# Output LayerNorm from the residual's accumulated sum and a squaring pass on ScalarE, biases by broadcast load, and another closing order

## What is computed

```
u     = h @ h.T / sqrt(384);  a = softmax(u);  delta = a * adj
attn  = delta / (sum(delta) + 1e-10)
ctx   = (attn * upper) @ (h @ Wl.T + bl) + diag(attn) * (h @ Ws.T + bs) + (attn * lower) @ (h @ Wr.T + br)
h     = relu(layernorm(ctx, eps=1e-12) * g + beta)
out   = layernorm(x + h_after_layer_2, eps=1e-5)       # no gain, no shift
```

## Time and profile before

| | |
|---|---|
| median of three runs | 1637.04 us (1635.62, 1637.04, 1637.73) |
| the profiled execution | 1637.5 us, span 1635.7 us |
| busy share PE, PEld, DVE, ACT, POOL | 98%, 98%, 91%, 58%, 73% |
| chain that ended last, by engine | PE 91%, DVE 2%, then DMA, POOL, SP's queue, ACT about 1% each |
| DMA | 178.61 MB, 43% of 16 engines |

### The profile page before, as it was taken

One profiled execution on the slowest core, in us unless ns is written; L12 is line 12 of the kernel. 1 busy time (PEld: TensorE's weight loads), 2 busy tenths in 40 slices (PEclk: granted clock), 3 DMA queues, 4 the chain that ended last, 5 costly groups with the idle time before them and its releaser, 6 DMA issues.

```text
span 1635.7 us, 35455 instructions
## 1 busy us (share of the span) xinstructions
PE 1609.5 (98%) x9505; PEld 1601.3 (98%) x9505; DVE 1491.4 (91%) x4628; ACT 951.4 (58%) x2451; POOL 1202.1 (73%) x1541
## 2 busy tenths in 40 slices
PE   8999999999999999999999999999999999999995
PEld 7999999999999999999999999999999999999995
DVE  7799999999999999999999999999999999999987
ACT  5565665556566556556656655665665556566553
POOL 5677777777777777777777777777777777777763
PEclk9999999999999999999999999999999999999998
DMA  4344444444444444444444444444444444444431
GB/s 158 94 116 107 111 111 112 106 113 114 107 114 109 111 107 113 114 107 114 110 110 107 112 115 107 114 111 110 108 111 115 107 114 111 110 109 110 114 83 44
DMA packets 463515, 178.61 MB, mean 109 GB/s; under 512 B 348545, under 2 KB 462593, under 8 KB 463490
## 3 DMA queue, kind: packets, MB, share of 16 engines
q1 hardware_dynamic: 463490, 178.32, 43.1%
HBM read 112.34 MB, written 65.86 MB: 109 GB/s over the span
## 4 chain that ended last, share of the span: by engine, by line
PE 91%; DVE 2%; DMA 1%; POOL 1%; SPq 1%; ACT 1%; issue 1%; DVEq 0%; POOLq 0%; ACTq 0%
PE p_proj L427 70%; PE p_gather L514 15%; PE p_score L421 5%; PE p_score L443 1%; DMA rows_mem<-rows_blocks 1%; DMA attnT_whole<-attn_mem 1%; SPq L366 1%; SPq L351 1%; POOL rstd L1164 0%; POOL proj_split L283 0%; POOL attnT L1154 0%; POOL attnT_split L1160 0%; DVE stats L626 0%; ACT normed L961 0%; DVE stats L672 0%
## 5 line engine op out<-in xcount | busy, mean ns | idle before, releaser
L427 PE MATMUL p_proj<-w,hT_layer 128*128 128x384 f32 x6912 | 1371.6, 339 | 0.2 <-DVE proj L697 0.2
L427 PEld LDWEIGHTS p_proj<-w,hT_layer 128*128 128x128 f32 x6912 | 1165.9, 189 | 0.5 <-DVE proj L697 0.5
L283 POOL TENSOR_TENSOR proj_split<-proj,proj_split 128x768 fp32r<-128x768 f32 x253 | 467.6, 1848 | 276.9 <-ACT proj_split L957 276.9
L957 ACT ACTIVATE proj_split<-proj 128x768 fp32r<-128x768 f32 x256 | 214.9, 839 | 394.9 <-DVE proj L697 393.8
L514 PE MATMUL p_gather<-proj_split,attnT_split 128*128 128x384 f32 x1536 | 309.2, 335 | 3.0 <-POOL attnT_split L1160 2.4
L514 PEld LDWEIGHTS p_gather<-proj_split,attnT_split 128*128 128x128 f32 x1536 | 270.0, 188 | 4.9 <-POOL attnT_split L1160 4.1
L1164 POOL TENSOR_TENSOR rstd<-veps,neg_half 128x1 f32<-128x1 f32 x384 | 211.2, 550 | 75.3 <-DVE veps L635 61.8
L697 DVE TENSOR_TENSOR proj<-p_proj,bias_all 128x768 f32<-128x768 f32 x256 | 245.1, 957 | 12.0 <-PE p_proj L427 4.4
L421 PE MATMUL p_score<-hT_layer 128*128 128x256 f32 x768 | 216.8, 283 | 2.0 <-DVE rows L729 2.0
L1154 POOL TENSOR_TENSOR attnT<-attnT_whole,sides 128x256 f32<-128x256 f32 x249 | 184.5, 741 | 41.0 <-DMA attnT_whole<-attn_mem 39.0
L1160 POOL TENSOR_TENSOR attnT_split<-attnT,attnT_split 128x256 fp32r<-128x256 f32 x256 | 190.3, 743 | 5.8 <-ACT attnT_split L948 5.8
(11 more groups left out here) (67 smaller groups left out, 1568.2 us busy)
## 6 DMA issues: line engine op xcount, KB each, us to landing
xt_raw<-xT SPq DMA_DIRECT2D x128, 192.0 KB, 2.5
xn<-x SPq DMA_DIRECT2D x128, 192.0 KB, 2.4
out<-o SPq DMA_DIRECT2D x128, 192.0 KB, 2.0
rows_mem<-rows_blocks SPq DMA_DIRECT2D x124, 192.0 KB, 1.9
rowsT<-rows_mem SPq DMA_DIRECT2D x496, 48.0 KB, 2.4
adj_layer<-adj SPq DMA_DIRECT2D x256, 64.0 KB, 1.9
attn_mem<-attn_blocks SPq DMA_DIRECT2D x124, 128.0 KB, 1.7
attnT_whole<-attn_mem SPq DMA_DIRECT2D x496, 32.0 KB, 2.2
```

What stands on the lines that cost most here:

```text
L283: op.tensor_tensor(proj_split[u][:, LO], proj[u][:, UP:LOW + 1, :], proj_split[u][:, HI].bitcast(F32), ALU.subtract).then_inc(s_proj_lo[k], 1)
L427: return nc.tensor.matmul(p_proj[:, which, 0:D], hT_of(k, b)[:, slot, st, c, :], w[:, k, which, mv, c, :], start=(n == 0), stop=(n == 8))
L957: nc.scalar.activation(proj_split[u][:, HI], proj[u][:, UP:LOW + 1, :], ACT.Copy).then_inc(s_proj_hi[k], 1)
```

## The change

The output statistics no longer come from bn_stats. The instruction that makes y also accumulates its sum per row; DVE scales that by -1/384 to the negated mean; ScalarE squares y + (-mean) with an accumulated sum and turns that into the variance plus epsilon. y gets two buffers, and `gathered` is no longer used for it. In the loop ScalarE runs the squaring where `finish` stood and `finish` after layer 2's cross scores; POOL's deviation for the output moves behind the one for layer 2. Both layers' biases are loaded with partition broadcasts, the sides' and the self bias apart, layer 1's behind its weights; the matmuls and copies that spread it go, and 9 warm matmuls run instead of 4. The closing steps have another order on DVE, ScalarE and POOL.

```diff
...
@@ -110,7 +108,11 @@
         normed = sb("normed", [P, D])
         stats6 = sb("stats6", [P, 3, 6])
         rows = [sb(f"rows{k}", [P, 4, COLS]) for k in (1, 2)]
-        y = sb("y", [P, D])
+        y = sb("y", [P, 2, D])
+        y_sum = sb("y_sum", [P, 1])
+        y_squares = sb("y_squares", [P, 1])
+        spread = sb("spread", [P, D])
+        out_eps = sb("out_eps", [P, 1])
 
 
 
...
@@ -317,12 +315,14 @@
         @block.sync
         def _(sp):
             sp.dma_start(xt_raw[:, 0], xT[0]).then_inc(s_xt[0], 16)
-            sp.dma_start(bias_row[:], bias[0:1]).then_inc(s_bias_row, 16)
             sp.dma_start(w_raw[:, 0, UP], WT[0, :, UP]).then_inc(s_w[0][UP], 16)
             sp.dma_start(adj_tile[0][:, 0], adj[0]).then_inc(s_adj[0][0], 16)
             sp.dma_start(w_raw[:, 0, LOW], WT[0, :, LOW]).then_inc(s_w[0][LOW], 16)
             sp.dma_start(xt_raw[:, 1], xT[1]).then_inc(s_xt[1], 16)
             sp.dma_start(w_raw[:, 0, SELF], WT[0, :, SELF]).then_inc(s_w[0][SELF], 16)
+            sp.dma_start(bias_all[:, 0, UP:LOW + 1],
+                         bias[0, UP:LOW + 1].partition_broadcast(P)).then_inc(s_bias_sides[0], 16)
+            sp.dma_start(bias_all[:, 0, SELF], bias[0, SELF].partition_broadcast(P)).then_inc(s_bias_self[0], 16)
             sp.dma_start(adj_tile[0][:, 1], adj[1]).then_inc(s_adj[0][1], 16)
             done(sp, s_lo[0], 0)
             sp.dma_start(xt_raw[:, 0], xT[2]).then_inc(s_xt[0], 16)
...
@@ -380,7 +380,10 @@
                         sp.dma_start(w_raw[:, 1, which], WT[1, :, which]).then_inc(s_w[1][which], 16)
                     sp.dma_start(gain1[:], gain_cols).then_inc(s_cols, 16)
                     sp.dma_start(shift1[:], shift_cols).then_inc(s_cols, 16)
-                    sp.dma_start(bias_all[:, 1], bias[1].partition_broadcast(P)).then_inc(s_bias2, 16)
+                    sp.dma_start(bias_all[:, 1, UP:LOW + 1],
+                                 bias[1, UP:LOW + 1].partition_broadcast(P)).then_inc(s_bias_sides[1], 16)
+                    sp.dma_start(bias_all[:, 1, SELF],
+                                 bias[1, SELF].partition_broadcast(P)).then_inc(s_bias_self[1], 16)
                     sp.dma_start(gain2[:], gain_row.partition_broadcast(P)).then_inc(s_const, 16)
                     sp.dma_start(shift2[:], shift_row.partition_broadcast(P)).then_inc(s_const, 16)
                 if live(i, i - 1):
...
@@ -518,13 +521,8 @@
 
 
             pe.wait_ge(s_warm, 1)
-            for n in range(4):
+            for n in range(9):
                 nc.tensor.matmul(p_gather[1][:, 0:N], warm[:], warm[:], start=True, stop=True)
-            pe.wait_ge(s_warm, 2)
-            pe.wait_ge(s_bias_row, 16)
-            for which, spread in enumerate((p_gather[0], p_gather[1], p_proj[:, 0])):
-                nc.tensor.matmul(spread[:, 0:D], ones_row[:], bias_row[:, which, :], start=True,
-                                 stop=True).then_inc(s_bias_spread, 1)
             pe.wait_ge(s_setup, 5)
             pe.wait_ge(s_ident_r, 1)
             pe.wait_ge(s_ident_p, 2)
...
@@ -659,23 +656,17 @@
                 done(dve, s_shifted, b)
                 moved(dve, s_xn, b, p)
 
-                done(dve, s_o, b - 1 if not isinstance(b, int) or b < G - 3 else b - 2)
-                nc.vector.scalar_tensor_tensor(out=y_rows(b), in0=ctx_rows(1, b), scalar=0.0,
-                                               in1=xn[:, p, :], op0=ALU.max,
-                                               op1=ALU.add).then_inc(s_y, 1)
-
-            def output_moments(b):
+                done(dve, s_o, b - 2)
+                nc.vector.scalar_tensor_tensor(out=y[:, p, :], in0=ctx_rows(1, b), scalar=0.0,
+                                               in1=xn[:, p, :], op0=ALU.max, op1=ALU.add,
+                                               accum_out=y_sum[:]).then_inc(s_y, 1)
+
+            def output_mean(b):
+
+                done(dve, s_y_nbias, b - 1)
                 done(dve, s_y, b)
-                if isinstance(b, int) and b >= G - 3:
-
-                    done(dve, s_y_nbias, b - 1)
-                nc.vector.bn_stats(stats6[:, 2], y_rows(b)).then_inc(s_y_stats, 1)
-                done_apart(dve, s_y_stats, b)
-                nc.vector.bn_aggr(moments[:, 2], stats6[:, 2]).then_inc(s_y_moments, 1)
-                done(dve, s_y_moments, b)
-                nc.vector.tensor_scalar(veps[:, 2:3], moments[:, 2, 1:2], OUT_EPS, None, ALU.add)
-                nc.vector.tensor_scalar(neg_mean[:, 2:3], moments[:, 2, 0:1], -1.0, None,
-                                        ALU.mult).then_inc(s_y_veps, 1)
+                nc.vector.tensor_scalar(neg_mean[:, 2:3], y_sum[:], -1.0 / D, None,
+                                        ALU.mult).then_inc(s_y_mean, 1)
 
             def low_rows(b, slot):
 
...
@@ -687,8 +678,8 @@
             def add_bias(k, b, sides_too):
 
                 u = unit(k, b)
-                if k == 1 and isinstance(b, int) and b == 0:
-                    dve.wait_ge(s_bias2, 16)
+                if isinstance(b, int) and b == 0:
+                    dve.wait_ge((s_bias_sides if sides_too else s_bias_self)[k], 16)
                 if sides_too:
                     if k == 0 and isinstance(b, int) and 0 < b < 4:
 
...
@@ -755,16 +746,11 @@
                                         ALU.subtract).then_inc(s_w_lo[k][which], 1)
 
             nc.vector.memset(warm[:], 0.0).then_inc(s_warm, 1)
-            nc.vector.memset(ones_row[:], 1.0).then_inc(s_warm, 1)
             dve.wait_ge(s_setup, 5)
             nc.vector.tensor_copy(ident_r[:], ident[:]).then_inc(s_ident_r, 1)
             for k in range(2):
                 nc.vector.tensor_copy(ident_p[k], ident[:]).then_inc(s_ident_p, 1)
-            for which, spread in enumerate((p_gather[0], p_gather[1], p_proj[:, 0])):
-                dve.wait_ge(s_bias_spread, which + 1)
-                nc.vector.tensor_copy(bias_all[:, 0, which], spread[:, 0:D]).then_inc(s_bias_copied, 1)
             dve.wait_ge(s_ident_p, 2)
-            dve.wait_ge(s_bias_copied, 3)
 
             for c in range(C):
                 low_weights(0, UP, c)
...
@@ -841,31 +827,31 @@
                     mask(i, 1, G - 3, 1)
                     diagonal(1, G - 3, 1)
                     output_rows(G - 5, 1)
-                    output_moments(G - 5)
                 elif i == G:
+                    output_mean(G - 5)
                     cut_sides(1, G - 3)
                     add_bias(1, G - 3, True)
                     done(dve, s_score[1], G - 2)
                     scaled_scores(1, G - 2, 0)
                     row_moments(1, G - 4, 0)
-                    low_rows(G - 1, 1)
+                    row_variance(1, G - 4, 0).then_inc(s_veps[1], 1)
+                    centre_layer2(i, G - 4)
                     mask(i, 1, G - 2, 0)
                     diagonal(1, G - 2, 0)
-                    row_variance(1, G - 4, 0).then_inc(s_veps[1], 1)
-                    centre_layer2(i, G - 4)
+                    low_rows(G - 1, 1)
                     add_bias(1, G - 3, False)
                     output_rows(G - 4, 0)
                 elif i == G + 1:
                     cut_sides(1, G - 2)
                     add_bias(1, G - 2, True)
-                    output_moments(G - 4)
+                    output_mean(G - 4)
                     done(dve, s_score[1], G - 1)
                     scaled_scores(1, G - 1, 1)
                     row_moments(1, G - 3, 1)
+                    row_variance(1, G - 3, 1).then_inc(s_veps[1], 1)
+                    centre_layer2(i, G - 3)
                     mask(i, 1, G - 1, 1)
                     diagonal(1, G - 1, 1)
-                    row_variance(1, G - 3, 1).then_inc(s_veps[1], 1)
-                    centre_layer2(i, G - 3)
                     add_bias(1, G - 2, False)
                 elif i == G + 2:
                     cut_sides(1, G - 1)
...
@@ -873,19 +859,19 @@
                     output_rows(G - 3, 1)
                     done(dve, s_proj_lo[1], G - 2)
                     low_projections(nc.vector, dve, 1, G - 1)
+                    output_mean(G - 3)
                     add_bias(1, G - 1, False)
                     row_moments(1, G - 2, 0)
                     row_variance(1, G - 2, 0).then_inc(s_veps[1], 1)
                     centre_layer2(i, G - 2)
-                    output_moments(G - 3)
                 elif i == G + 3:
                     row_moments(1, G - 1, 1)
                     row_variance(1, G - 1, 1).then_inc(s_veps[1], 1)
                     centre_layer2(i, G - 1)
                     output_rows(G - 2, 0)
+                    output_mean(G - 2)
                     output_rows(G - 1, 1)
-                    output_moments(G - 2)
-                    output_moments(G - 1)
+                    output_mean(G - 1)
 
             def iteration(i, p):
                 q = 1 - p
...
@@ -916,7 +902,7 @@
                 done(dve, s_score[1], i - 2)
```

(49 more changed lines are left out.)

17 lines of the change are left out of this document (6 added, 11 removed).

## The result

The changed kernel took 1631.23 us (median of 7, 1629.76 to 1631.82) beside 1636.32 us for the kernel before on the same chip: ratio 0.9965, 95% interval 0.9954 to 0.9977. Part of the miss is the base: the forecast was taken off 1637.04, and the kernel before measured 0.7 lower here. The profiled execution took 1631.82 us for a span of 1630.1 (before 1637.5 and 1635.7), so 5.6 us are to be found in the two traces.

What follows compares the result with a forecast made beforehand. The prediction took PE to bound the loop at 12.44 us a tile, leaving gains only at the two ends. From 1637.04 us, −0.5 −0.3 −2.0 = −2.8 gave 1634.2 us; range 1631.8 to 1636.3.

Steps and rivals of the forecast that it cites:

- the term of the opening: Start of the kernel: removing bias matmuls, copies and row load was to save 0.5 us, bounds 0 and 0.85 plus half-speed matmuls.
- the slot it leaves in SP's queue I count at nothing: Opening: dropping the bias row load from SP's queue was counted as worth 0.
- about 8.3: Opening: forecast start in us of the first projection, from 9.17, 0.85 us earlier.
- If PE's clock rises when it did: Opening: with the clock rising at the same time, the sides' end would move by 0.46 us only.
- Rival 1: Opening: longer warm row raises the clock before the projections; opening −1.8 to −2.0, total 1632.8 us; chance 0.28.
- Loop, 0: Loop tiles: PE stays busy throughout at 12.44 us a tile, so DVE's relief gains nothing.
- Rival 2: Loop: squaring and variance hold ACT over 2.2 us, PE waits; each 0.1 us over costs 12 us; chance 0.08.
- Early tile, −0.3: The early 13.43 us tile, a DMA chain, was to gain 0.3 us; ends 0 and 0.99.
- rival 4: Early tile and two at the loop's end lose DMA waits: −1.0 more, 1633.2 us; chance 0.10.
- Closing, −2.0: Tiles 122 to 127: tile 127's rows 1.2 us earlier on DVE, tail 0.8 shorter; ends −1.0 and −2.6.
- PE 0.1 late there: Closing: tile 127's low rows, now behind mask and diagonal, were to make PE 0.1 us late.
- Rival 3: Closing gives half, −1.0, with the opening at −0.3: 1635.7 us; chance 0.12.

Runs made afterwards that it cites:

- e1: Kernel before with the new opening alone (nine warm matmuls, broadcast bias loads, no row load, no spreading), old statistics and closing order: 1633.35 us, ratio 0.9981.
- e4: Changed kernel with the old load of layer 1's bias row back second in SP's queue, its data unused: 1630.88 us, ratio 0.9972.
- e2: Changed kernel with the old opening put back (row load, ones-row matmuls and copies, four warm matmuls), new statistics and closing order kept: 1632.85 us, ratio 0.9983.
- e3: Changed kernel with four warm matmuls in place of nine, nothing else: 1631.17 us, ratio 0.9968.
- e12: Changed kernel with VectorE's old closing order back in two tiles, a repeat run, statistics still on ScalarE: 1629.74 us, ratio 0.9966.
- e7: Changed kernel with one more squaring pass on ScalarE in every loop tile, its result unused: 1631.56 us, ratio 0.9975.
- e9: Changed kernel with four warm matmuls and three unused one-row spreading matmuls behind them, no row load or copies: 1632.68 us, ratio 0.9984.
- e8: Changed kernel with three more squaring passes on ScalarE in every loop tile, their results unused: 1641.27 us, ratio 1.0039.
- e10: Changed kernel with one exchange of VectorE's closing order undone (tile 127's low rows, tile 126's mask and diagonal before tile 124's variance and centring): 1630.02 us, ratio 0.9966.
- e6: Changed kernel with the output's statistics and variance back on VectorE, new opening, orders and second y buffer kept: 1632.54 us, ratio 0.9981.
- e11: Changed kernel once more, unaltered, beside the kernel before on the same chip: 1630.94 us, ratio 0.9970.

## Why the prediction was wrong, point by point

**What failed is the term of the opening, "−0.5".** It was 2.5 us by e1's median, and 2.2 by the gathers that open the loop. Three parts of its working were off:
- "the slot it leaves in SP's queue I count at nothing": the weights' rounding starts 0.8 us sooner without it (e4). I had let the cross copy follow roundings that began at 6.47, so "about 8.3" for the first projection became 7.24. That the copy stands right behind three roundings was right, and where they start was not. By e4 this part is worth 0.5 at the first gather and next to nothing at the end.
- "If PE's clock rises when it did": it did not. By the spacing of the matmuls the projections turned fast near 13.4 us before and near 14 in e2, near 11 in e3 and e12, at 10.3 in e7, between 11 and 12 in e9, and in the changed kernel they were fast from the start. I took half of the earlier start away for a clock that would stay slow till 13.4, so that the sides' end would move by 0.46. It moved by 2.6 (the matmul behind the 18 projections starts at 11.80 instead of 14.37), and still by 2.3 in e3 (12.04), at the lower clock. The bound is another one: the first gather now hangs on the landing of LOW, 9.5 us ahead of it, and came 1.75 sooner.
- The transfers' chain at 43 to 51 us: the sum had no term for it, and it gave 0.66 more by the fifth gather. The tiles behind that took 0.2 back.

The larger part is what the prediction named without pricing it by itself: PE's own 4.2 us of one-row matmuls ahead of the scores. It let the first projection gain only what roundings from 6.47 allowed, 0.85; e9, with roundings from 5.27, shows that these matmuls alone keep it at 8.92.

**Rival 1** named the right size of the opening, −1.8 to −2.0, and 1632.8 for the whole, and the wrong cause, so its number came near by luck. The first projections did run at the full clock in the changed kernel, and "the weights hold PE back after that" was right; but four warm matmuls and half the clock give the same time. The Trainium skill (TensorE: Matmul & The Clock Gate, Part 1) has activity release the clock. Nine full warm matmuls were followed by fast projections in the changed kernel (9 in 1.78 us) and by slow ones in e12 (18 in 5.02 us), so the rule alone does not say what this opening gets.

**Loop, 0:** right. 12.44 us, PE busy throughout, DVE at 86% (about 85 forecast), ACT at 66% (about 65). The squaring pass took 602 ns, its accumulator read 187, the variance 295, as the lines of the changed kernel show for 128 tiles:

```profile
L993 ACT ACTIVATE spread<-y,neg_mean 128x384 f32<-128x384 f32 x128 | 77.1, 602 | 4.7 <-DVE neg_mean L668 4.7
...
L998 ACT ACTIVATE veps<-y_squares,out_eps 128x1 f32<-128x1 f32 x128 | 37.7, 295 | 4.1
L993 ACT ACTIVATION_READ_ACCUMULATOR spread<-y,neg_mean 128x1 f32 x128 | 23.9, 187 | 0.0
...
L1005 ACT ACT_TABLE_LOAD x1 | 1.3, 1283 | 0.8 <-PEq L1329 0.8
```

0.6, 0.19 and 0.28 were forecast, no table load was added, and the 1.1 us of slack are there (e7 takes 0.4 of them free, e8 uses them up). Rival 2's mechanism is real and begins there, but its point, 2.2 us, was read off one tile and is too low: from the start of the squaring to PE's matmul it is 2.77 us in the middle one of the loop's tiles (2.18 to 2.86) and the matmul needs 0.31 of it behind the copy's start, which leaves 2.46. e8 holds ACT 2.45, right at it, so its price of 12 us for each 0.1 us over stands untested.

**Early tile, −0.3:** wrong but small. 12.77 us instead of 13.43, then tiles of 13.01 and 12.65 that were not there. In e1, with the old statistics, this tile took 12.44 and in e10 too. Which tile waits for its turned rows changes from profile to profile, so the earlier trace rows's 13.43 was no property of the kernel, and rival 4's loosening neither; the time from the fifth gather to the nineteenth is 87.2 to 88.8 us, whatever the statistics (before 88.5, changed 88.7; e8, with three passes more, has 89.2).

**Closing, −2.0:** right as far as it went. Relative to the gather that opens the closing, which starts 2.67 us sooner, tile 127's rows come 1.4 us sooner on DVE (1618.69 against 1622.74, less 2.67; −1.2 forecast) and the last output pass ends 2.0 sooner (1627.74 against 1632.41, less 2.67). The tail between them gave 0.6 where 0.8 was forecast (9.05 us for 9.67; the steps listed sum to 8.8, not 8.9), so that the 2.0 is met by two small errors that cancel. The chain that ended last, in the changed kernel, its issue times left out:

```profile
1622.21 0.16 DVE neg_mean L668
1622.39 0.72 ACT spread L993 x2
1623.13 0.30 ACT veps L998
1623.51 0.56 POOL rstd L1173
1624.13 0.20 POOL nbias L1177
1624.41 0.71 ACT o L947
1625.12 0.61 ACT spread L993 x2
1625.75 0.30 ACT veps L998
1626.12 0.55 POOL rstd L1173
1626.71 0.24 POOLq L63
1627.03 0.71 ACT o L947
```

From the mean to the end of the last pass it is 5.5 us, where the prediction's steps sum to 5.4; against the earlier trace rows, DVE's two statistics are out of it. The 0.9 us more came behind the last pass, in the store, which the prediction took as fixed. 0.6 of it goes with the statistics (e1 and e6, 2.98), the other 0.3 only the profile of the kernel before has. Within the 2.0 the order had a wrong sign: "PE 0.1 late there" for tile 127's low rows was 0.73. Rival 3, the closing at half, is out.

The forecast's own numbers: with 2.2 for the opening in place of 0.5 (the early tiles' loss is in it), 0 for the early tile, and 2.0 and 0.9 for the closing, the sum is 5.1. The two traces have 5.6, with the 0.5 of the loop's last tiles; the medians have 5.1, and 4.3 in e11. That the sum meets the first of these exactly is luck. The range let rival 1 come together with one more microsecond, not with the base's 0.7 as well.

## What to carry to other kernels

A setup step that is spread over engines is paid on the engine whose queue it shares with the first real work: ask what stands behind it there (here the scores, behind 4.2 us of one-row matmuls), not only who waits for its result. Do not take away part of an earlier start for a stretch at TensorE's lower clock that is assumed to end when it did; ask first what the next stage will wait for once the start is earlier (here the second piece of the weights). A range should let two terms reach their far ends together. Waits on DMAs that one profile shows should be looked for in a second one before a change is credited with them.
